# Row maxima of a 16-head attention: 128 query columns at a time, taken across heads, and one shared 64-row product for the rest

## The reference, cut to what matters

```python
qh, kh, vh = proj(q, Wq, bq), proj(k, Wk, bk), proj(v, Wv, bv)     # 16 heads of 8
scores = jnp.einsum('bhqd,bhkd->bhqk', qh, kh) / sqrt(8)           # 16 x 100 x 1444 per batch
attn = jax.nn.softmax(scores, axis=-1)
out = jnp.einsum('bhqk,bhkd->bhqd', attn, vh)
x = x + jnp.tanh(g) * (concat(out) @ Wo.T + bo)
# the last attention: no biases, and scores of keys at or past valid_lens are set to -1e6 before the softmax
```

## Time and profile before

| what | us |
|---|---|
| median of 3 runs | 5916.65 (5912.44 to 5920.44) |
| profiled execution, its own time | 5889.56 |
| its span | 5887.6 |
| PE busy in the span | 5295.7 (90%) |
| DVE busy in the span | 4177.3 (71%) |
| ACT busy in the span | 3119.9 (53%) |
| POOL busy in the span | 1529.0 (26%) |
| mean granted TensorE clock | 0.948 |

### The profile page before, as it was taken

How to read it: one execution, slowest core, us unless ns; L and a number is a source line. 1 busy time by engine, 2 the same in 40 slices (tenths; PEclk the granted TensorE clock), 3 DMA queues, 4 the chain that set the end, 5 groups by cost and what they waited for, 6 DMA issues and landing times. The chain is left out here.

```text
span 5887.6 us, 111451 instructions
## 1 busy us (share of the span) xinstructions
PE 5295.7 (90%) x39878; PEld 3446.4 (59%) x39878; DVE 4177.3 (71%) x11750; ACT 3119.9 (53%) x4492; POOL 1529.0 (26%) x1162
## 2 busy tenths in 40 slices
PE   6999999997949999999999978889358999999996
PEld 3666666665835555555555548767345665565653
DVE  6778787786756766666676667746457777878785
ACT  3666666665624444444444445534235666666664
POOL 2222222221432222222222215501432222222220
PEclk9999999998969999999999989989668999999998
DMA  3333233332224332333333225387323323323230
GB/s 80 72 73 80 67 77 77 71 72 61 63 73 96 81 76 73 81 80 75 79 81 73 70 53 101 68 230 221 92 73 79 74 67 73 71 68 76 67 72 13
DMA packets 160573, 475.27 MB, mean 81 GB/s; under 512 B 34714, under 2 KB 85717, under 8 KB 159832
## 3 DMA queue, kind: packets, MB, share of 16 engines
q1 hardware_dynamic: 148704, 449.52, 32.1%
q0 software_dynamic: 11328, 18.72, 1.1%
HBM read 237.50 MB, written 19.88 MB: 44 GB/s over the span
## 5 line engine op out<-in xcount | busy, mean ns | idle before, releaser
L850 PE MATMUL a_max<-a_stack,a_qblk 96*100 96x482 f32 (+1 forms) x4608 | 2003.3, 455 | 112.9 <-DVE a_mx L671 35.0
L550 ACT ACTIVATE a_probs<-a_scores 128x800 f32<-128x800 f32 (+1 forms) x1536 | 1281.2, 838 | 1015.4 <-PE a_scores L867 652.3
L863 PE MATMUL a_scores<-a_qblk,a_stack 128*128 128x400 f32 (+1 forms) x4608 | 1378.0, 372 | 5.9 <-POOL a_qblk L455 2.9
L665 DVE CUSTOM_DVE_ANT_0 a_dump<-a_max,a_mqf 100x482 f32<-100x482 f32 (+1 forms) x1536 | 978.3, 657 | 425.9 <-PE a_max L850 394.9
L850 PEld LDWEIGHTS a_max<-a_stack,a_qblk 96*100 96x100 f32 x4608 | 767.2, 167 | 743.9 <-issue 206.1
L671 DVE CUSTOM_DVE_ANT_0 a_dump<-a_max,a_penq 100x482 f32<-100x482 f32 (+1 forms) x1536 | 955.4, 657 | 274.9 <-PE a_max L850 253.7
L657 DVE TENSOR_REDUCE a_mx<-a_max 100x1 f32<-100x482 f32 (+1 forms) x1536 | 941.5, 654 | 259.0 <-PE a_max L850 241.2
L879 PE MATMUL a_pv<-a_probs,a_v_aug 128*32 128x200 f32 x18432 | 1052.4, 340 | 3.4 <-ACT a_probs L548 2.1
L863 PEld LDWEIGHTS a_scores<-a_qblk,a_stack 128*128 128x128 f32 (+1 forms) x4608 | 840.1, 186 | 181.4 <-issue 52.6
L548 ACT ACTIVATE a_probs<-a_scores,a_kbias 128x800 f32<-128x800 f32 (+1 forms) x768 | 697.6, 926 | 405.8 <-PE a_scores L863 405.5
L879 PEld LDWEIGHTS a_pv<-a_probs,a_v_aug 128*32 128x32 f32 x18432 | 458.6, 108 | 476.0 <-issue 309.6
(11 more groups left out here) (473 smaller groups left out, 6285.3 us busy)
## 6 DMA issues: line engine op xcount, KB each, us to landing
a_stack<-a_khi SPq DMA_DIRECT2D x768, 180.5 KB, 3.4
a_ctxT<-in_ctxT_dram SPq DMA_DIRECT2D x128, 722.0 KB, 14.0
a_stack<-a_klo SPq DMA_DIRECT2D x384, 180.5 KB, 3.5
f_wb<-weights_by_token SPq DMA_DIRECT2D x16, 1600.0 KB
a_ctxn<-in_ctxn_dram SPq DMA_DIRECT2D x32, 704.0 KB
a_mt_i<-in_mask1T_dram SPq DMA_DIRECT2D x32, 600.0 KB
a_mq_i<-in_mask_dram SPq DMA_DIRECT2D x32, 564.1 KB
a_mask_i<-in_mask_dram SPq DMA_DIRECT2D x32, 541.5 KB
```

The source lines that it names most:

```text
L550: act.activation(out_, in_, ACT.Exp, scale=scale).then_inc(sc_free, 1)
L665: nc.vector.tensor_tensor_reduce(dump[:, k % 2, 0:n], src, mqf[:, b % 2, o:o + n], 1.0, -3.0e38, ALU.mult, ALU.max, out_).then_inc(mx_free, 1)
L850: pe.matmul(to[0:S, 0:n], qblk[0:96, b % 2, HALF * h + head, :], stack[0:96, b % 2, g, o:o + n], start=True, stop=True).then_inc(mx_full, 1)
L863: ins = pe.matmul(out_, stack[:, b % 2, 2 * h + g, kt * D:kt * D + r], qblk[:, b % 2, HALF * h + 4 * g:HALF * h + 4 * g + 4, :].rearrange( ...
```

## The change

a0 and a3 call a new function, `packed_attention_phase`; a1 still calls `attention_phase`. The new function is a copy without the mask's parts, and differs in these:

- The 400 columns of a group are cut into 3 blocks of 128 columns, across the borders of heads, and 16 columns that are left (the last 16 queries of the group's last head). A batch has 4 x 3 x 3 = 36 products with 128 columns of weights.
- The 4 x 16 left columns of the groups share one product of 64 rows: `qleft` has 64 columns for each group, zero but for the 16 of that group, and 4 matmuls add up in one PSUM bank. There are 3 of these (one for each chunk of keys), 12 matmuls, in units 8, 12 and 16 of the batch before.
- DVE reduces 36 + 3 = 39 products for each batch, not 48. `mx` has 7 columns for each half, one of them for the left rows; the second half copies it (`L1419` in the new kernel).
- `neg_turn` turns 128 columns, not 100.
- POOL has `q_left`, one instruction of 96x64 for each batch, and `neg_spread` is two instructions.
- An even unit has 2 max products, an odd unit 1. Before scores begin, 24 max products and the 3 shared ones are made, where it was 32 max products.

The core of the diff:

```diff
+PACKED = 3
+LEFT = 4 * S - PACKED * D
+PACKED_LEAD = 3 * LEAD // 2
+LEFT_AT = (8, 12, 16)
...
+        def fulls_at(b, u):
+            k = MAX_JOBS * 2 * b + PACKED_LEAD + u + (u + 1) // 2
+            return (k, k + 1) if u % 2 == 0 else (k,)
...
+            def q_left(b):
+                if b > 0:
+                    full(pool, "left", b - 1, NCH - 1)
+                to = qleft[:, :].rearrange("p (g n) -> p g n", g=GROUPS)[:, :, 0:LEFT]
+                pool.tensor_tensor(to, qs[:, :, S - LEFT:S].bitcast(F32), bc(bc(blk[0:96, 3], 1, GROUPS), 2, LEFT),
+                                   ALU.mult).then_inc(qleft_ready, 1)
...
+                pool.tensor_tensor(to[:, :, 0:PACKED * D].rearrange("p g (j m) -> p g j m", j=PACKED),
+                                   bc(bc(nsb[96:128, :], 1, PACKED), 1, 2),
+                                   bc(blk[96:128, at:at + 2 * PACKED].rearrange("p (g j) -> p g j", g=2), 3, D), ALU.mult)
+                pool.tensor_tensor(to[:, :, PACKED * D:4 * S],
+                                   nsb[96:128, 2 * LEFT * h:2 * LEFT * (h + 1)].rearrange("p (g n) -> p g n", g=2),
+                                   bc(bc(blk[96:128, at + 2 * PACKED], 1, 2), 2, LEFT), ALU.mult).then_inc(qneg_ready, 1)
...
+                g, j = 2 * h + block // PACKED, block % PACKED
+                at = 4 * S * g + D * j
+                pe.matmul(to[:, 0:n], qblk[0:96, b % 2, at:at + D], stack[0:96, b % 2, g, o:o + n],
+                          start=True, stop=True).then_inc(mx_full, 1)
...
+                for g in range(GROUPS):
+                    ins = pe.matmul(to[0:GROUPS * LEFT, 0:n], qleft[:, GROUPS * LEFT * g:GROUPS * LEFT * (g + 1)],
+                                    stack[0:96, b % 2, g, o:o + n], start=(g == 0), stop=(g == GROUPS - 1))
+                ins.then_inc(mx_full, 1)
...
-            attention_phase(nc, "a0", x, xnT, ident, w, dram, DK ** -0.5, gates[0:S, 0:1])
+            packed_attention_phase(nc, "a0", x, xnT, ident, w, dram, DK ** -0.5, gates[0:S, 0:1])
...
-            attention_phase(nc, "a3", x, xnT, ident, w, dram, DK ** -0.5, gates[0:S, 3:4], lens=A["lens"])
+            packed_attention_phase(nc, "a3", x, xnT, ident, w, dram, DK ** -0.5, gates[0:S, 3:4], lens=A["lens"])
```

620 lines of the change are left out of this document (added).

## The result

The changed kernel takes **5900.43 us** (median of 9 runs, 5889.97 to 5906.45) where the kernel before, run beside it, takes 5914.47 (5908.43 to 5922.77). The medians are 14 us apart. The ratio of the runs is 0.9968, with a 95% interval of 0.9959 to 0.9977, which is 19 us less. The forecast was 64 less. The sign is right, the size is not, and the time lies outside the range.

What follows compares the result with a forecast made beforehand. PE's own work was taken to set a0, with some 2.5 us a batch of bank waits in a3; a0 unchanged, a3 -58 us, openings -6, together -64 from the median: 5853 us, range 5805 to 5895.

Steps and rivals of the forecast that it cites:

- So I let the bank waits go, in a0 wholly, in a3 but for 0.15: Units 2 to 7 walked through: PE's waits for banks that DVE frees, some 2.5 us a batch in a3, nearly vanish.
- The sum for a3: a3 up to unit 19 was to take 33.69 us where it was 35.41, then 6.84: 1.89 less a batch.
- DVE sets the pace: Before the first scores, 27 reductions instead of 32 were to save 2.9 us, twice, so 6 us.
- What bounds a0: PE's own work sets a0's period of 40.63 us; DVE costs it about 0.5 us a batch.
- widths: Weights of 128 columns, not 100, cost 0.02 us at each of 12 exposed loads, 0.2 a batch.
- POOL is late next: Units 19 to 24: scores of unit 24 wait for POOL's spread maxima, 6.65 us in a0, 6.84 in a3.
- rival 1: POOL's chain isn't in the way: units 19 to 24 cost 6.0 us, another 43 us less, 5810; 8%.
- ACT. The wait of unit 17 goes: Left matmuls of unit 16 stand ahead of unit 17's scores, removing their wait for ACT: 0.37 us less in a0.
- DVE's relief: The profile after was to show DVE busy some 5 us a batch less.
- the wait for POOL: Scores of unit 0 were to show PE idle some 0.5 us for POOL's spread, in nearly every batch of both stages.
- no max product of a3 waits for DVE: The profile after was to show no idle before a3's max products for DVE.
- rival 4: DVE stalls go only by half, left reductions and penalty row meeting in the 3-bank ring; 31 us stays, 5884; 9%.

## Why the prediction was wrong in size, and what of it held

By the periods the miss, against the 64 us of the forecast, is made of these: a3 41.82 and not 40.58, 1.24 x 31 = 38 us; a0 40.79 and not 40.63, 5 us; and what stands before the first scores, 6 us. That is 49 of the 64, which leaves 15.

- **"So I let the bank waits go, in a0 wholly, in a3 but for 0.15"**: this is the step that failed. In a0 it held. In a3 bank waits of 16 us remain over the middle 1150, in every batch, 0.38 a batch for the penalty row alone and about 0.5 in unit 8. Three parts of the step were wrong. I took the 2.5 us of waits in a3 for a matter of DVE's load, and 0.86 of them were the place of the penalty row, which the change leaves as it is. I walked through units 2 to 7 and stopped one unit short: in unit 8 the negation, the output projection and the new left products meet in the ring. And I took bank waits by DVE's backlog alone, not by which bank an instruction needs.
- **The sum for a3** was 1.44 too little in units 0 to 19. By the runs, 0.38 is the row and 0.47 unit 8 (0.62, less the 0.15 that the projection took in any case); about 0.2 is ACT's exponential, and 0.37 what a0 shows too. That makes 1.42. The parts were measured in different kernels and overlap somewhat, so the sum is no proof that nothing else is in it.
- **"DVE sets the pace" before the first scores**, 2.9 us less in each stage: this failed too. To the first scores it was 0.9 less in a0 and 1.1 more in a3, and other kernels with the same opening have 40.5 to 41.8 and 42.4 to 43.9, against 41.8 and 42.7 before. DVE waits for PE there, which has 36 matmuls of maxima and left rows to do where it had 32. No run changed only this, so its cause stays open. DVE in a0:

```profile
77.22 2.35 DVE L1404 TENSOR_REDUCE a_mx<-a_max 128x1 f32<-128x480 f32 x4 [1.00 <-PE a_max L1567]
```

- **What bounds a0** (PE's own work): right as to the size, with some luck. Its period moved by 0.16 of 40.63 because two misses cancel, 0.37 too little up to unit 19 and 0.22 too much behind it. The 0.37 are small terms: left products at 0.92 and not 0.88 (3 x 0.04), widths 0.24 and not 0.20, the values' projection in unit 9 1.81 to the next product where it took 1.70, and slot waits of units 12 and 14 some 0.1. I read these off the median distances; only the widths were tried by themselves. (The prediction calls 12 x 0.024 the same sum as its 0.2; it is 0.29, and 0.24 was measured.)
- **POOL is late next**: right in place and in mechanism, shown by the run that changes its order. In size 0.2 too dear in each stage: I added 0.10 for a weight load behind POOL, but the scores start 0.06 after it, their load 0.01 before them; the two spreads overlap by 0.04; and the wider turn of the maxima, 0.05, stands beside POOL's chain and not on it. PE's wait there was put at 0.6 in a0 and is 0.40. That to be rid of this wait is worth 44 us, more than all the change brought, was in rival 1 (43 us).
- **"ACT. The wait of unit 17 goes"**: right, and the left products of unit 16 are what fills it, as the run that moves them shows. But I asked of ACT only this. The scores of units 12 and 14, where a projection holds the second slot, now wait longer, in a3 0.86 behind their max product in unit 14 where it was 0.64; the plain exponential gives back 0.29 a batch in a3.
- **Signs**: of those that I had named, DVE's relief, a0's period and the wait for POOL came true. That no max product of a3 waits for DVE did not, nor a3's period near 40.6.
- **Rivals**: rival 4, that DVE's stalls go only by half, is nearest to what happened. It had 9%, and would have left 1 us of a3's 1.9; 1.24 was left. It names the penalty row and the left products in the ring of 3, and both do wait there, but at two places and the left products behind the negation, not behind the row. It was priced by halving, with no walk behind the number.

## What to carry to other kernels

Before work is taken from an engine to relieve a stall, ask whether the stall comes from its load or from one long instruction at a bad place; in a3, moving that one instruction of 0.97 us won 0.86 us a batch, and cutting 9 of 48 reductions, as the change does it, 0.69. A gain that reaches a wait of its own (here POOL's order, worth nothing in the kernel before with its row moved, and 44 us in the changed one) is only had if that wait is moved in the same change. Where products share a ring, write down for each product which earlier one frees its bank: here a product of 0.15 us that takes a turn cost another 0.4.

## What the hardware showed unexpectedly

- Left products that stand behind value products and in front of a max product save the exposed weight load after it: 4 left matmuls take 0.92 there and the scores behind the next max product then come in 0.22, where they come in 0.33 without; behind scores the same 4 take 0.87 and nothing behind them gets shorter.
- Two POOL instructions of one chain, 32x768 and 32x32 elements, start 1.43 apart where the first is shown as 1.47 long; from the first's start to the second's end it is 1.67, where the one spread of 32x800 took 1.52, so splitting it cost 0.15.
